# Attention and FFN block on one core: exponentials turned in 32x32 blocks by VectorE and moved by DMA instead of turned by TensorE

## What is computed

```python
q, k, v = x @ Wq, kv[..., :1024], kv[..., 1024:]        # 16 heads of 64, kv = x @ Wkv
s = einsum('bhid,bhjd->bhij', q * 64 ** -0.5, k)          # 1024 x 1024 for each head
gm = max(s, axis=-1)                                      # over the whole row, masked part too
p = where(causal_mask, 0.0, exp(s - gm))
out = einsum('bhij,bhjd->bhid', p, v) / (sum(p) + 1e-8)
x = layernorm(x + out @ Wo + bo)
r = sigmoid(xr @ W_r); out = r * (relu(xk @ W_k) ** 2 @ W_v)   # xr, xk mix x with the token before
x = layernorm(x + out)
```

## Time and profile before

| | us |
|---|---|
| median of 3 runs (lowest, highest) | 1263.78 (1261.5, 1263.96) |
| the profiled execution, its own time | 1263.72 |
| its span in the profile | 1261.9 |

### The profile page before, as it was taken

How to read it: one execution, slowest core, us unless ns; L and a number is a source line. 1 busy time by engine, 2 the same in 40 slices (tenths; PEclk the granted TensorE clock), 3 DMA queues, 4 the chain that set the end, 5 groups by cost and what they waited for, 6 DMA issues and landing times.

```text
span 1261.9 us, 22548 instructions
## 1 busy us (share of the span) xinstructions
PE 1192.6 (95%) x8051; PEld 794.7 (63%) x8051; DVE 911.8 (72%) x1780; ACT 770.9 (61%) x1730; POOL 490.8 (39%) x838
## 2 busy tenths in 40 slices
PE   6899999999999999999999999999999999999654
PEld 4666666666666666666666666666666666665343
DVE  5777777777777777777777777776777777777597
ACT  4666656666666566666666666666666666665254
POOL 4344444444444444444444444444444444442100
PEclk9999999999999999999999999999999999999887
DMA  4000000000000000000000000000000000000001
GB/s 140 18 2 18 17 18 18 18 18 18 2 18 18 18 18 19 18 18 1 18 18 18 18 18 18 18 2 18 17 19 18 18 18 18 2 18 18 17 18 50
DMA packets 25038, 24.98 MB, mean 20 GB/s; under 512 B 10464, under 2 KB 20448, under 8 KB 24928
## 3 DMA queue, kind: packets, MB, share of 16 engines
q1 hardware_dynamic: 24352, 23.14, 7.0%
q10 hardware_dynamic: 576, 0.39, 0.1%
HBM read 21.17 MB, written 2.36 MB: 19 GB/s over the span
## 4 chain that ended last, share of the span: by engine, by line
PE 78%; DVE 13%; issue 7%; DMA 1%; ACT 0%; POOLq 0%; POOL 0%; DVEq 0%; SPq 0%
PE ps_s L688 33%; PE ps_x L720 20%; PE ps_x L736 13%; DVE tile L509 8%; PE ps_x L625 6%; PE ps_x L747 4%; DVE stats L542 1%; PE ps_x L634 1%; DVE pt L564 1%; DVE tile L553 1%; DVE y L553 0%; DVE tile L608 0%; DMA pt<-in_L_attn_x 0%; DVE tile L605 0%; DMA rb<-recips 0%
## 5 line engine op out<-in xcount | busy, mean ns | idle before, releaser
L509 DVE TENSOR_SCALAR_CACHE_REDUCE tile<-ps_s 128x1024 f32<-128x1024 f32 x512 | 606.5, 1222 | 299.6 <-PE ps_s L688 297.2
L397 ACT ACTIVATE tile<-tile,neg_max 128x640 f32<-128x640 f32 (+7 forms) x512 | 396.4, 778 | 227.6 <-POOL tile L315 226.9
L688 PE MATMUL ps_s<-ks,qs 64*128 64x512 f32 x3072 | 427.0, 410 | 21.4 <-DVE tile L509 18.0
L315 POOL TENSOR_SCALAR_AFFINE_SELECT tile<-tile 128x128 f32<-128x128 f32 x512 | 149.7, 293 | 661.1 <-DVE tile L509 661.1
L688 PEld LDWEIGHTS ps_s<-ks,qs 64*128 64x128 f32 x3072 | 271.7, 185 | 134.2 <-DVE tile L509 77.0
L720 PEld LDWEIGHTS ps_x<-ident,tile 128*128 128x128 f32 x2304 | 259.1, 140 | 89.8 <-issue 68.0
L720 PE MATMUL ps_x<-ident,tile 128*128 128x128 f32 x2304 | 306.6, 276 | 0.1
L736 PE MATMUL ps_x<-pt,vs 128*64 128x512 f32 (+3 forms) x1536 | 269.9, 493 | 0.1
L410 ACT ACTIVATE pt<-ps_x 128x384 f32<-128x384 f32 (+3 forms) x384 | 165.8, 493 | 118.2 <-PE ps_x L720 118.2
L736 PEld LDWEIGHTS ps_x<-pt,vs 128*64 128x64 f32 x1536 | 102.2, 137 | 160.0 <-issue 150.8
L522 DVE COPY pt<-ps_x 128x384 f32<-128x384 f32 (+3 forms) x384 | 190.6, 546 | 2.6
(11 more groups left out here) (66 smaller groups left out, 443.3 us busy)
## 6 DMA issues: line engine op xcount, KB each, us to landing
rb<-recips SPq DMA_DIRECT2D x64, 256.0 KB, 3.9
out<-y SPq DMA_DIRECT2D x4, 512.0 KB, 3.2
y<-in_L_attn_x SPq DMA_DIRECT2D x3, 512.0 KB, 8.5
pt<-in_L_attn_Wkv SPq DMA_DIRECT2D x2, 384.0 KB, 6.8
pt<-in_L_attn_x SPq DMA_DIRECT2D x2, 256.0 KB, 4.4
wos<-in_L_attn_Wo SPq DMA_DIRECT2D x1, 512.0 KB, 7.1
recips<-recips_sb SPq DMA_DIRECT2D x32, 8.0 KB, 1.5
pt<-in_L_attn_Wq SPq DMA_DIRECT2D x1, 384.0 KB, 6.0
```

What stands on the lines that cost most here:

```text
L315: pool.affine_select(out=block_of, in_=block_of, compare_op=ALU.is_ge, fill=fill, base=0, pattern=[[-1, P]], channel_multiplier=1).then_in ...
L397: act.activation(cols, cols, ACT.Exp, bias=neg_max[:, at:at + 1], scale=-1.0, accum_out=sums[:, p % 2, a, t:t + 1]).then_inc(s_exp, 1)
L509: dve.tensor_scalar(tile[:, at, :], ps_s[a][:, :], -SCALE, None, ALU.mult, ALU.min, accum_out=neg_max[:, at:at + 1]).then_inc(s_evac, 1)
L688: ins = mm(ps_s[a][:, c * HALF:(c + 1) * HALF], qs[rows, p % 2, qh, t * P:(t + 1) * P], ks[rows, p % 2, kh, c * HALF:(c + 1) * HALF], star ...
```

## The change

What it does:

- The exponentials are no longer turned on PE. DVE turns each tile in 32x32 blocks, SBUF to SBUF, into a staging buffer (`stage`, one instruction for each tile and head, `turn_tile`), in the step after the tile's scores were taken. A turn in 32x32 blocks leaves each block in the partition group of 32 where it came from; SP then moves the blocks to their places in `pt` with 16 DMAs for each **unit** of two tiles (256 queries), `move`: 64 DMAs for each pair, each 32 partitions x 4 rows of 64, 128, 192 or 256 floats (units 0 to 3). Two staging buffers: units 0 and 2 share one, units 1 and 3 the other.
- Both copies `take_turned` (ACT L410, DVE L522) go.
- P*V goes by the four units of 256 queries instead of two of 512; the blocks of P that are used, and so the columns that PE streams, are the same.
- PSUM: three score places (`NSCORES = 3`) that go round by slot, and two shared banks. `scores` waits for one more evacuation fewer: only for head 0 of the step before.
- `add_out` moves from DVE to POOL, behind a new ACT copy of the projection to `ot` (`take_out`). `take_values` has three pieces instead of two.
- `RING` 6 to 4, `XSLOTS` 3 to 2. The steps of the q, k, v and output projections are rearranged.

Core of the diff:

```diff
-RING = 6
-XSLOTS = 3
+RING = 4
+XSLOTS = 2
...
+UNITS = TILES // 2
+UNIT_COLS = [(2 * u + 2) * 32 for u in range(UNITS)]
+MOVED = 16 * 16
...
-QK_AT = {0: 0, 1: 1, 3: 2, 5: 3}
-V_AT = 1
+QK_AT = {1: (0, 1), 3: (2,), 6: (3,)}
+SPLIT_AT = {1: 0, 2: 1, 4: 2, 6: 3}
+V_AT = {1: 0, 3: 1}
-OUT_AT = {3: 0, 7: 1}
-NORM_AT = {2: 0, 6: 1}
-TURN_AT = {0: ((1, 7),), 1: ((0, 0),), 3: ((0, 1), (0, 2)), 5: ((0, 3), (0, 4)), 7: ((0, 5), (0, 6))}
-PV_BEFORE = {2: (0, 1, 2), 4: (3, 4, 5, 6, 7)}
-PV_OWN = {6: (0, 1, 2, 3)}
+OUT_AT = {6: 0, 7: 1}
+NORM_AT = {3: 0, 5: 1}
+
+PV_AT = {0: ((0, 0, (0, 1)), (0, 1, (0, 1, 2, 3))), 2: ((1, 2, (0, 1, 2, 3, 4, 5)),),
+         4: ((2, 3, (0, 1, 2, 3)),), 5: ((2, 3, (4, 5, 6, 7)),)}
...
+            def move(p, u):
...
+                at_least(sp, s_pv, 3 * (p - 1) + PV_DONE[u])
+                sp.wait_ge(s_turned, SLOTS * p + 4 * u + 4)
+                for a in range(4):
+                    for b in range(4):
+                        sp.dma_start(pt_unit(u)[32 * b:32 * b + 32, :, a, :], stage_unit(u)[32 * a:32 * a + 32, :, b, :]
+                                     ).then_inc(s_moved[u], 16)
...
+            for p in range(ALL_PAIRS + 1):
+                if p > 0:
+                    spread_recips(p - 1)
+                    move(p - 1, 3)
+                if p < ALL_PAIRS:
+                    for u in range(3):
+                        move(p, u)
...
+            def turn_tile(p, t, a):
+                u = t // 2
+                if t % 2 == 0 and a == 0:
+
+                    at_least(dve, s_moved[(u + 2) % UNITS], MOVED * (p + u // 2))
...
+                dve.wait_ge(s_exp, SLOTS * p + 2 * t + a + 1)
+                dve.transpose(stage_unit(u)[:, 2 * a + t % 2, :, 0:32 * (t + 1)],
+                              tile[:, slot_of(p, t, a), 0:(t + 1) * P].rearrange("p (j b k) -> p b j k", b=4, k=32)
+                              ).then_inc(s_turned, 1)
...
-                    if t in OUT_AT and p > 0:
-                        add_out(p - 1, OUT_AT[t])
-                    for q, u in turned_in(p, t):
-                        take_turned(q, u)
+                    q, u = (p, t - 1) if t > 0 else (p - 1, TILES - 1)
+                    if 0 <= q < ALL_PAIRS:
+                        turn_tile(q, u, 0)
+                        turn_tile(q, u, 1)
...
-                at_least(pe, s_evac, SLOTS * p + 2 * t)
+                at_least(pe, s_evac, SLOTS * p + 2 * t + 2 - NSCORES)
...
-            def turn_tile(p, t, a):
-                pe.wait_ge(s_exp, SLOTS * p + 2 * t + a + 1)
...
-                        ins = turn(ps_t[BANK[unit]][:, b, :], tile[:, slot_of(p, t, a), (j + b) * P:(j + b + 1) * P],
-                                   ident[:, :])
-                    ins.then_inc(s_turned[a], 1)
...
+                if js[0] == 0:
+                    pe.wait_ge(s_moved[u], MOVED * (p + 1))
...
+                        moving = pt_unit(u)[:, 2 * a + second:2 * a + 2, :, 32 * j:32 * j + 32]
+                        ins = mm(bank[a * DH:(a + 1) * DH, cols + second * P:cols + 2 * P],
+                                 vs[:, p // 2 % 2, j, p % 2, a * DH:(a + 1) * DH], moving,
+                                 start=(j == 0), stop=(j == final))
```

More of the change, by code:

```diff
@@ L136, in build @@
         recips = sb("recips_sb", [P, 2, 2, TILES])
-        pt0 = sb("pt0", [P, 2, 4, HALF])
-        pt1 = sb("pt1", [P, 2, 8, HALF])
+        stage = [sb(f"stage{n}", [P, cols]) for n, cols in enumerate(STAGE_COLS)]
+        pt = sb("pt", [P, 16 * sum(UNIT_COLS)])
         ot = sb("ot", [P, N])
@@ L192, in build @@
         s_exp = sem("s_exp")
-        s_turned = [sem("s_turned0"), sem("s_turned1")]
-        s_pt = [sem("s_pt0"), sem("s_pt1")]
+        s_turned = sem("s_turned")
+        s_gaps = sem("s_gaps")
+        s_moved = [sem(f"s_moved{u}") for u in range(UNITS)]
         s_pv = sem("s_pv")
@@ L262, in _, with spread_recips @@
             sp.dma_start(small[:, 1:2], mu_k.rearrange("(p a) -> p a", a=1)).then_inc(s_small, 16)
-            for p in range(ALL_PAIRS):
+            def move(p, u):
+                if p == 0 and u == 0:
+                    sp.wait_ge(s_gaps, 2)
+                if p == 0 and u == 2:
+                    sp.wait_ge(f_wt, 1)
+                if p == 0 and u == 3:
+                    sp.wait_ge(s_wlo, 3)
+                    sp.wait_ge(s_w0lo, 3)
+                at_least(sp, s_pv, 3 * (p - 1) + PV_DONE[u])
[4 more added lines that the diff above has]
+                                     ).then_inc(s_moved[u], 16)
+            def spread_recips(p):
                 sp.wait_ge(s_recip, p + 1)
@@ L289, in _ @@
             fill = pool.to_reg(MASKED)
+            for n in range(2):
+                pool.memset(stage[n][:, :], 0.0).then_inc(s_gaps, 1)
             pool.wait_ge(s_wraw, 48)
@@ L323, in norm, with add_out @@
                                    ALU.mult).then_inc(s_norm, 1)
-            for p in range(ALL_PAIRS + 1):
+            def add_out(p, c):
+                b = p // PAIRS
+                cols = y[:, b * N + c * HALF:b * N + (c + 1) * HALF]
+                pool.wait_ge(s_outc, 2 * p + c + 1)
+                pool.tensor_tensor(cols, cols, ot[:, c * HALF:(c + 1) * HALF], ALU.add).then_inc(s_yadd, 1)
+            for p in range(ALL_PAIRS + 2):
                 for t in range(TILES):
@@ L398, in exp_of @@
                                accum_out=sums[:, p % 2, a, t:t + 1]).then_inc(s_exp, 1)
[L400 to L411, removed]
             def take_qk(p, n):
@@ L432, in _, with take_out @@
+            def take_out(p, c):
+                act.wait_ge(s_out, 2 * p + c + 1)
+                act.activation(ot[:, c * HALF:(c + 1) * HALF], ps_x[BANK["out", p, c]][:, :], ACT.Copy
+                               ).then_inc(s_outc, 1)
             for p in range(ALL_PAIRS + 1):
                 for t in range(TILES):
[L434 to L437, removed]
@@ L447, in _ @@
+                    if t == 7 and p > 0:
+                        take_out(p - 1, 0)
+                    if p + 1 < ALL_PAIRS and t in QK_AT:
+                        take_qk(p + 1, QK_AT[t][0])
+                    if t in V_AT and p < ALL_PAIRS:
+                        take_v(p // 2, 2 * (p % 2) + V_AT[t])
+                    if p + 1 < ALL_PAIRS:
+                        for n in QK_AT.get(t, ())[1:]:
+                            take_qk(p + 1, n)
                     if t == X_AT and p < ALL_PAIRS:
```

266 lines of the change are left out of this document (112 added, 154 removed).

## The result

The changed kernel takes **1595.49 us** (median of 4 runs, 1593.41 to 1596.82) against 1263.49 (4 runs): the ratio is 1.263, 95% interval 1.2608 to 1.2652. It is 332 us slower. The forecast was 1183, the range ended at 1320.

A forecast was written before the change was run, and what follows sets the result against it. SP's queue was taken as the bound, at 33.4 us a pair, above PE with DVE at 31.0. 51.5 + 31 x 33.4 + 94.1 + 1.8 = 1183 us; range 1105 to 1320, about 0.82.

The forecast's parts named there:

- The issue of a move: SP's queue: 0.48 us for each of 64 moves a pair, 30.7 us, bounds 0.41 and 0.56.
- The rows from an SBUF source are the short ones: SP's queue: argument against slow issues, from 32 SBUF-to-DRAM DMAs issued in 0.37 us.
- the reciprocals: SP's queue: issuing their DMAs and waiting for the landing, 2.7 us a pair with a gap.
- SP is slow: Rival, SP's queue: from 0.52 us an issue the kernel becomes slower; 1304 us at 0.54, 1343 at 0.56; chance 0.26.
- the first interval: Start of the kernel, before the first reciprocals' DMA: 55.5 becomes 51.5 us, 0 to 6 less.
- the tail: End of the kernel, after the last pair's reciprocals' DMA: 91.1 becomes 94 us, 0 to 8 more.
- PE and DVE: Steps of a pair: with a third score place the two together need 31.0 us, including 0.3 for joints between queues.
- The block turns: DVE: each tile's turn priced like a copy, 0.094 + 0.126n us for n blocks, 10.6 us a pair.
- dear-turns rival: DVE: block turns cost twice a copy, 19.7 us a pair, period 39.8, time 1381 us; chance 0.08.
- The buffers: Staging buffers: deep enough that SP never idles; unit 3 ready at 31.8, asked for at 33.4 us, perhaps landing late.
- The small-transfer rule: Moves: skill's advice to join transfers under 64 KB; unit 0's are 32 KB, said to change nothing in the sum.
- The clock: TensorE: slower matmuls behind a PE wait, 1.3 us more in the first pair; none counted for the rest.

The follow-up runs named there:

- e6: e4 with 16 more small DMAs a pair on SP, four of each of four kinds, behind unit 1's moves; 1101.16 us.
- e4: Changed kernel with 48 of the 64 moves of a pair left out; 1101.45 us.
- e2: Changed kernel with 32 of the 64 moves of a pair left out; 1107.12 us.
- e7: Complete kernel with e1's layout, ACT issuing 4 of each unit's 16 moves and SP 12; 1339.44 us, ratio 1.0604 to the kernel before.
- e3: Changed kernel with head 1's half of every move left out, still 64 moves a pair; 1570.28 us.
- e1: Changed kernel with staging buffer and pt laid out so each move is one contiguous run per partition; 1561.54 us, ratio 1.2361 to the kernel before.
- e12: e11's staging and P*V order with e8's split of the issues (SP 10, ACT 4, GpSimd 2); 1184.29 us, ratio 0.9387 to the kernel before.
- e11: e7 with staging handed round so unit 3 no longer shares with the next pair's unit 1, its P*V whole in step 5; 1273.92 us (three runs).
- e8: e7 with GpSimd also issuing 2 of each unit's 16 moves, SP 10; 1305.07 us, ratio 1.0334 to the kernel before.
- e9: e7 with each unit's 16 moves reordered so that moves in flight together read different partition groups; 1335.07 us, ratio 1.0582 to the kernel before.

## Why the prediction was wrong

- **The issue of a move, the step that failed.** The prediction bounded it by 0.41 and 0.56 and took 0.48, between a DMA from SBUF to DRAM (0.37) and loads from DRAM (0.47 to 0.54). Measured: 0.60 and a gap, 0.65 from start to start, 0.68 in the mean. Neither end of that range was an end. The 0.54 of the `rb` pair is the mean of a first one at 0.45, behind a pause, and a second at 0.59, right behind it: the trace before already had a price of 0.59 for an issue behind its like, and the moves come 64 in a row. "The rows from an SBUF source are the short ones" was read as speaking for cheap moves; those rows stood behind a pause and went to DRAM. The same DMA takes 0.54 behind the moves, and e6 has 0.17 us more for SBUF on both sides than for DRAM on one, at the same bytes. 64 x (0.65 - 0.48) = 10.9 us of the 13.0 that the period is above 33.4; the long issues, 64 x 0.03, are 1.9; the reciprocals took 3.05 where 2.7 was summed, and their DMA itself rose from 0.37 to 0.54 behind the moves.
- **The mechanism** was the one forecast: SP's queue is the bound, the rival "SP is slow" is its case, and its turning point of 0.52 us stands. 31 x 46.39 in place of 31 x 33.4 is 403 of the 412 us missed; the first interval (57.6 against 51.5) and the tail (95.9 against 94.1) are most of the rest.
- **The range.** A cost that no row showed, multiplied by 64 x 32 = 2048, was given bounds from other kinds with 0.02 us of room above. Every 0.01 us of it is 20 us of time; 0.02 of room is no bound for a form that was never measured, and the range ended at 0.55, inside even the bound of 0.56 that the prediction gave itself.
- **PE and DVE**: right. 31.0 forecast, 31.0 in e2, and 1108 against 1107.12 us; that it fits to the tenth has some luck in it, since 0.3 of it was an allowance for joints. The block turns: 290 ns for one block and 1191 for eight, where 290 and 1172 were priced. The dear-turns rival fell: after the first block each further one took (1191 - 290)/7 = 129 ns. The Trainium skill's page "VectorE: DVE Perf Modes" gives, under "The three transpose paths", 311 ns for a block in 16-bit elements; the 290 ns of one block here, in float32, are near it, the further ones are not.
- **The buffers.** "Each is in time, by little" was worked out for moves that land 1.6 us after the last issue and for 300 GB/s. With SP at 46 us it did not decide, but e7 shows that it would have been the next bound: the full DMA engines moved some 230 GB/s, and unit 3 was late by 5 to 7 us. The prediction let that be "a microsecond or two".
- **The small-transfer rule.** The Trainium skill's page "DMA: Bandwidth & Descriptors", "Rules for kernel authors", would have transfers under 64 KB joined. Fewer DMAs would have been right here, but not because of their size: moves of 32 KB and of 128 KB took the same 0.60 us to issue, and halving every move (e3) saved 25 us of 1595. It is the number that counts, and the prediction dismissed the rule with "the overhead counted here is the issue", at too low a price. The same page of the Trainium skill says under "Issuing engines are not separate DMA queues" that a second issuing engine saves only sequencer time, usually small beside the transfer. Here that time was the bound: from e1 to e7 it is 222 us.
- **The clock.** I counted nothing. The granted clock was 0.88 in the mean, with stretches at 0.50 behind waits of 7 to 8 us. With SP 81% of the chain and PE 3% this cost next to nothing; e12 has 0.971.

## What to carry to other kernels

Count the DMAs that a queue must issue in a period before their bytes, and price them by a row with the same two sides that stands right behind its like; a mean over a pair, or a DMA behind a pause, is no such row. Where no row has them, the bound is open, and a probe with a few DMAs of the kind, behind what will stand before them, measures it. When a queue is the bound, spread the issues over the queues that have time, and look next at when each transfer must have landed: handing the buffer to the piece that can best wait was worth 65 us from e7 to e11 and 121 from e8 to e12. A part of a change that fails can hide one that works: leaving out half of the costly part (e2) showed what the rest was worth.

## What was not expected of the hardware

- Behind its like, a DMA with SBUF on both sides took SP 0.59 to 0.60 us to issue, whether it moved 64 bytes or 4 KB a partition, on 32 partitions or 128. With DRAM on one side it took 0.42 in e6, but 0.59 as the second `rb`, and 0.54 to 0.59 when it stood right behind a move; the reciprocals' DMA had 0.37 behind a pause.
- Full DMA engines moved 232 GB/s over 12 us of moves in pieces of 4 KB (e7) and 231 in the other order (e9), against 300 for loads of mostly 512-byte pieces. With pieces of 1 KB, in the changed kernel, they were not quite full and moved 211 at a share of 0.88.
- The ACT queue's DMA issues ran beside ACT's computing: in e7 two moves were issued in 1.20 us within and after a 1.15 us exponential:

```profile
699.96 1.15 ACT L442 ACTIVATE tile<-tile,neg_max 128x1024 f32<-128x1024 f32 x1
700.00 1.20 ACTq L171 DMA_DIRECT2D pt<-stage  x2
```

- Two moves issued by GpSimd took 1.0 us of its time together (e8), less than the two on SP. The profile counts this as busy time of GpSimd, where it does not for SP and ACT.
